# Attention norms over three engines, GpSimd's constants behind the norm, and a hint on the loop's back edge

## The reference

```python
def _layernorm(x, axis=-1, eps=1e-05):
    m = jnp.mean(x, axis=axis, keepdims=True)
    v = jnp.var(x, axis=axis, keepdims=True)
    return (x - m) / jnp.sqrt(v + eps)
...
    x = x + _L2_ffn_ref(_layernorm(x, axis=-1), L2_ffn_Wq, L2_ffn_bq, ...)
```

```python
        qkv = jnp.einsum('bsd,ed->bse', x, W_qkv)
        ...
        q = _rope(q, positions)
        k = _rope(k, positions)
        scores = jnp.einsum('bhqd,bhkd->bhqk', q, k) / jnp.sqrt(jnp.float32(dk))
        causal = jnp.tril(jnp.ones((S, S), dtype=bool))
        scores = jnp.where(causal[None, None, :, :], scores, -jnp.inf)
        attn = jax.nn.softmax(scores, axis=-1)
        out = jnp.einsum('bhqk,bhkd->bhqd', attn, v)
```

## Time and profile before

| | us |
|---|---|
| runs shown | 5552.94, 5564.20, 5540.51; median 5552.94 |
| profiled execution, its own time | 5545.3 |
| its span in the trace | 5543.6 |
| mean clock granted to TensorE | 0.921 of full speed |

### The profile page before, as it was taken

The page is one execution under the profiler, slowest core; times in us unless marked ns, Lnnn a source line. Parts: engine busy times, 40 slices in busy tenths (PEclk is TensorE's granted clock), DMA queues, the critical chain, the costliest instruction groups (busy, mean ns, idle before and its releaser), DMA issues. The chain is left out here.

```text
span 5543.6 us, 69676 instructions
## 1 busy us (share of the span) xinstructions
PE 4726.4 (85%) x22038; PEld 2207.0 (40%) x22038; DVE 3555.6 (64%) x8259; ACT 2738.1 (49%) x5070; POOL 1481.6 (27%) x1876
## 2 busy tenths in 40 slices
PE   4689887988879888898878988789887998989888
PEld 2134344443444324443244433444334543444344
DVE  5766856678556785667755587656865568456545
ACT  2255553555526554365542755435644455436453
POOL 2712620136101461105501064010730117200200
PEclk8889998999989999899989999999988999999789
DMA  3411310123101231012210132001320113101000
GB/s 130 146 35 60 115 62 1 47 67 107 53 3 54 73 110 35 3 54 92 91 34 4 53 113 84 20 23 45 119 74 13 35 50 118 67 2 54 1 27 6
DMA packets 150524, 315.98 MB, mean 57 GB/s; under 512 B 16208, under 2 KB 24912, under 8 KB 150112
## 3 DMA queue, kind: packets, MB, share of 16 engines
q1 hardware_dynamic: 150128, 311.17, 17.4%
HBM read 307.89 MB, written 3.21 MB: 56 GB/s over the span
## 5 line engine op out<-in xcount | busy, mean ns | idle before, releaser
L196 PE MATMUL BANKS<-WB 128*128 128x512 bf16 x1616 | 454.3, 433 | 194.1 <-DVE XN L440 56.5
L758 POOL TENSOR_TENSOR heads_work<-heads_work,heads_c_all 128x512 f32<-128x512 f32 x384 | 487.2, 1271 | 380.5 <-DVE heads_work L792 367.9
L1503 ACT ACTIVATE heads_prob<-BANKS 128x512 f32<-128x512 f32 (+3 forms) x768 | 377.3, 518 | 289.4 <-PE BANKS L1398 283.5
L212 POOL TENSOR_TENSOR rstd<-rstd,WF 128x4 f32<-128x4 f32 x24 | 24.2, 1007 | 1665.9 <-DVE rstd L230 1665.9
L725 PE MATMUL BANKS<-heads_work,WF 128*128 128x512 f32 x768 | 444.2, 664 | 0.4
L196 PEld LDWEIGHTS BANKS<-WB 128*128 128x128 bf16 x1616 | 166.7, 108 | 443.0 <-issue 216.7
L1398 PE MATMUL BANKS<-heads_parts_kT,heads_parts_qT 64*128 64x512 bf16 (+3 forms) x768 | 240.5, 363 | 69.3 <-DVE heads_nmax L1544 46.9
L405 POOL TENSOR_TENSOR rstd<-rstd,WF 128x4 f32<-128x4 f32 x48 | 48.5, 1010 | 936.7 <-DVE rstd L426 935.9
L2143 ACT COPY attn_probt<-BANKS 128x512 f32<-128x512 f32 x384 | 223.9, 583 | 126.1 <-PE BANKS L2069 123.7
L2164 DVE CUSTOM_DVE_ANT_0 attn_biased<-BANKS,attn_toep 128x512 f32<-128x512 f32 x384 | 263.1, 685 | 33.5 <-DMA attn_toep<-bias_line 20.4
L1541 DVE CUSTOM_DVE_ANT_0 BANKS<-BANKS,WF 128x384 f32<-128x384 f32 (+3 forms) x512 | 243.1, 503 | 64.0 <-PE BANKS L1398 60.9
(11 more groups left out here) (891 smaller groups left out, 10594.6 us busy)
## 6 DMA issues: line engine op xcount, KB each, us to landing
heads_c_all<-bc_rows SPq DMA_DIRECT2D x384, 256.0 KB, 3.2
heads_b_all<-bc_rows SPq DMA_DIRECT2D x192, 256.0 KB, 3.5
attn_toep<-bias_line SPq DMA_DIRECT2D x96, 448.0 KB, 4.3
last_x_w<-in_w SPq DMA_DIRECT2D x48, 512.0 KB, 3.6
s_c_all<-bc_rows SPq DMA_DIRECT2D x64, 256.0 KB, 3.3
yheads_c_all<-bc_rows SPq DMA_DIRECT2D x64, 256.0 KB, 3.2
s_b_all<-bc_rows SPq DMA_DIRECT2D x32, 256.0 KB, 3.6
yheads_b_all<-bc_rows SPq DMA_DIRECT2D x32, 256.0 KB, 3.5
```

What stands on the lines that cost most here:

```text
L196: nc.tensor.matmul(bank, ident_b, bc(ident_b[:, 0:1], [P, SEQ]), start=True, stop=True)
L758: nc.gpsimd.tensor_tensor(work[:, m % RW, :], work[:, m % RW, :], c_all[:, m % RC, :], ALU.mult).then_inc(rd, 1)
L1503: nc.scalar.activation(prob[:, i % PR, lo:hi], bank("T", i)[:, lo:hi], ACT.Exp).then_inc(exped, 1)
```

## The change

There are three parts. The two norms of the heads stage get `scaled_by_act=True`: VectorE only subtracts the mean, right behind the eps addition and with no wait for `rooted`, and sets a new semaphore `centred`; ScalarE waits for `centred` and `rooted` and multiplies the four tiles in place by `rstd`. The five memsets of the first attention get the due time of the projection, and wait for `ready`. And the loop is built with `hint_back_edge=True`.

```diff
@@ -392,11 +392,12 @@
             due[i] = next(streams[i], None)
 
     def norm_parts(st, tag, src, dst, small, at, dst_t=None, banks=None, rms=False, sq=None, gain_t=None, gain=None,
-                   shift=None, after=None, spare=None, idle=0, later=()):
+                   shift=None, after=None, spare=None, idle=0, later=(), scaled_by_act=False):
 
         s_stats, s_mv, s_rstd = small
         ch, normed, turned = st.sem(f"{tag}_chain"), st.sem(f"{tag}_normed"), st.sem(f"{tag}_turned")
         shifted, rooted, ready = st.sem(f"{tag}_shifted"), st.sem(f"{tag}_rooted"), st.sem(f"{tag}_ready")
+        centred = st.sem(f"{tag}_centred") if scaled_by_act else None
         HALF = SEQ // 2
 
         def gpsimd(pool):
@@ -424,9 +425,14 @@
                     last = V.bn_aggr(s_mv[:, j, :], s_stats[:, j, :])
                 link(last)
                 V.tensor_scalar(s_rstd[:, :], s_mv[:, :, 1], EPS, None, ALU.add).then_inc(shifted, 1)
-            yield at + 3.2
-            dve.wait_ge(rooted, 1)
-            for j in range(NJ):
+            if scaled_by_act:
+                for j in range(NJ):
+                    last = V.tensor_scalar(dst[:, j, :], src[:, j, :], s_mv[:, j, 0:1], None, ALU.subtract)
+                last.then_inc(centred, 1)
+            else:
+                yield at + 3.2
+                dve.wait_ge(rooted, 1)
+            for j in range(0 if scaled_by_act else NJ):
                 if rms:
                     ins = V.tensor_scalar(dst[:, j, :], src[:, j, :], s_rstd[:, j:j + 1], None, ALU.mult)
                 else:
@@ -464,6 +470,12 @@
         def scalar(act):
             if dst_t is None:
                 return
+            if scaled_by_act:
+                yield at + 3.2
+                act.wait_ge(centred, 1)
+                act.wait_ge(rooted, 1)
+                for j in range(NJ):
+                    nc.scalar.activation(dst[:, j, :], dst[:, j, :], ACT.Copy, scale=s_rstd[:, j:j + 1]).then_inc(normed, 1)
             yield at + 4.4
             act.wait_ge(turned, NJ // 2)
             if gain_t is not None:
@@ -1248,7 +1260,8 @@
                 pool.wait_ge(ready, 2)
                 nc.gpsimd.memset(parts[:, :, 0, :, SK:SM], 0.0).then_inc(blank, 1)
             else:
-                yield at - 5.0
+                yield at
+                pool.wait_ge(ready, 2)
                 nc.gpsimd.memset(vals[:, :, :, HD + 1:], 0.0)
                 nc.gpsimd.memset(vals[:, :, :, HD], 1.0)
                 nc.gpsimd.memset(parts[:, :, 0, :, SK:], 0.0)
@@ -1619,7 +1632,7 @@
                 ("a2", W("qkv2"), None, True, W("o2"), X, None),
                 ("a3", W("qkv3"), bqk_b, False, W("o3"), XN, W("bo3"))):
             ln = norm_parts(st, f"{tag}_ln", X, XN, SMALL, at, dst_t=XT, banks=(RING[1], RING[0]), after=before,
-                            spare=WEIGH, idle=10)
+                            spare=WEIGH, idle=10, scaled_by_act=True)
             rope = rope_parts(st, tag, ln.ready, w_qkv, bias, raw, RING, WEIGH, at + 6.0, bool(layers))
             head = head8_parts(st, tag, rope, heads, causal, O, RING, WEIGH, at + HEADS_AT, u)
             back = back_parts(st, f"{tag}_pb", head, O, ot[:, 0, :], w_o, add_to, RING, head.end + 0.5, bias=bias_o)
@@ -2243,7 +2256,7 @@
                 run(block, *streams)
 
     n = out.shape[0]
-    with nc.Fori(0, n - 2) as b:
+    with nc.Fori(0, n - 2, hint_back_edge=True) as b:
         layers(b, True, True)
     prefix[0] = "y"
     layers(n - 2, True, False)
```

## The result

| | kernel before | changed kernel |
|---|---|---|
| median of the first comparison, us | 5554.8 | 5481.6 |
| ratio, 95% interval | | 0.9867 (0.9840 to 0.9894) |
| median of a second comparison, us | 5540.7 | 5483.4 |
| ratio, 95% interval | | 0.9883 (0.9864 to 0.9902) |
| span of the profiled execution, us | 5543.6 | 5477.8 |

The account below looks back on a forecast made before the run. No engine is full, so hand-overs set the time. Hint 16.5, first norms 11.1, second norms 6.7 and clock 2 sum to 36.3 us, taking the median from 5552.9 to 5516 us, range 5502 to 5540.

Parts of the forecast that it names:

- The hint: Loop's five taken back edges: the branch hint saves 3.3 us at each, 16.5 us, bounds nothing to 17.5.
- First norms: Eight norms ahead of the first attention: projection 6.5 us after the statistics, gaining 11.1 us, bounds 5.6 to 24.
- the transposes start at about 4.9 ... whichever way the first step goes: First norm: TensorE's queue ends at 4.85 us, so pow and subtractions, side by side or in turn, leave projection at 6.5.
- Second norms: Eight norms ahead of the second attention: 7.7 us from seven, 1.0 lost in the last, sum 6.7, bounds 0.8 to 13.8.
- so I take 1.1: Second norm: pow and subtractions wait for each other, L1264 starts at 5.7 us, gain 1.1 us in each of seven.
- L1264 starts near 4.8: Second norm, case not taken: pow and subtractions run side by side, scaled tiles complete at 3.95 us, gain 2.0 us.
- I take +2: Clock term for the eight slow projections after a norm: a shorter TensorE stand gives back 2 us in all.
- bound of 13 for the clock: Upper bound of the clock term: up to 1.6 us per first norm, 13 us in all.
- the clock gives much more: Rival: slow projections go, 13 us in place of 2, some second norms side by side: 5503 us; chance 0.07.
- The late memset chain: Rival: moved memsets make mamba's L758 late, seven stages lose 3.7 us each: 5562, or 5579 without the hint; chance 0.05.
- The hint does nothing: Rival at the taken edges: the hint has no effect, 19.8 us are left, 5533 us; chance 0.16.
- the norms give nothing: Rival in the stages after norms: mamba waits or clock take back earlier projections, only the hint stays, 5536 us; chance 0.12.

Follow-up runs that it names:

- the scratch tiles: Kernel before with ScalarE scaling, memsets unmoved, no hint, plus four unread two-pointer VectorE tiles ahead of the subtractions; no total time given, tiles took 339 to 344 ns.
- the idle products: Kernel before with more than 10 idle products: 16 ahead of both norms, 5504.4 us, 0.9927; 22 in both, 0.9937; 22 in the second alone, 0.9942.
- their own kernels: Kernel before with the hint alone: 5524.9 us, 0.9984; changed kernel without the hint: 5485.6 us, 0.9914.

## Why the prediction missed

**The hint: right, with a remainder.** 14.9 us at the five taken edges against 16.5 forecast. The remainder behind it (about 5 us longer experts and bias attention) was not in the sum; the kernel as a whole gained 9 (0 to 18).

**First norms: the floor was read in one iteration and used for all.** The step that failed is "the transposes start at about 4.9 ... whichever way the first step goes". The 4.85 is the end of TensorE's queue in the first iteration, where the ten idle products ran at the low clock and took 4.42 us. Elsewhere in the kernel before three of the eight took 2.34, and after the change five of eight did. There the transposes follow ScalarE's tiles and the projection starts at 4.9, not 6.5: 5 × 1.65, with 2.3 us from the other three, is the 10.5 that were missing. The trace before holds the durations of all eight groups; the forecast rests on one.

**Second norms: the wrong one of two cases.** The step that failed is "so I take 1.1": L433 waits for whole GpSimd instructions beside it, and I put pow among these. The change and the scratch tiles show that pow on 128x4 holds nothing: 339 to 344 ns each beside it. The 3329 ns of the earlier trace rows stood beside five memsets in a row, none over 1.33 us; beside mamba's products L433 took up to 1431 ns. Neither says anything of pow. The other case of the same paragraph, "L1264 starts near 4.8", is what came, 4.83; counted to L1264, as the forecast did, the eight norms gave 13.3. The case that was taken also has a slip: 3.75 + 1.35 and the 0.85 that the first case puts behind its tiles are 5.95 and not 5.7, a gain of 0.85 and not of 1.1. The last sequence lost 0.2 us, the better end of 0.2 to 1.1. ScalarE's four tiles took 1.28 us, against 1.35.

**The clock: a term of 2 that was too small, and at the wrong place.** The step that failed is "I take +2", worked out for the products of the first norms alone. The four last rows of the table are −15.1 in one pair of executions and +4.1 in the other. So the size of the term is not known to better than that; on the medians 10 to 23 us are left beside edges and norms. The first attention can't carry it: in the sixteen profiled executions it lies between 834 and 862 us, and kernels with the old and with the new first norm overlap. What holds is the stretch behind the second norm, of which the forecast said nothing. It is 13.5 and 14.8 us shorter in the two executions; it took 2636 to 2656 us in the four kernels with the old norm and 4 or 10 products there, 2629 to 2638 in the five executions with the new one and 5 or 10, and 2601 to 2622 in the six with 16 or 22. The low-clock time in it fell from 498 to 464 us. From the first expert stage to the last store it fell from 772 to 687, and 43 of these 85 us lie in the norms and at the edges themselves. The sum's bound of 13 for the clock had the right size by luck, since it too was worked out for the first norms. That such a gain needs no earlier projection is shown by the idle products: they leave the second norm as long as it was, within 1.3 us in the sum of eight, and give 32 to 40 us. The rival of 0.07, "the clock gives much more", was nearest in kind and in size, and still 21 us short.

**The rivals.** The late memset chain fell with the memsets alone. "The hint does nothing" and "the norms give nothing" fell with their own kernels.

**What stays open.** The two edits and the idle products both shorten TensorE's stand in the second norm, and both remove its low-clock time. Between 4 and 10 products the stand shrinks by 1.30 us and next to nothing is gained, between 10 and 16 by 1.31 us, and 40 us are. Whether that step lies in the length of the stand or in the run of products ahead of it isn't shown: both change together, and no run takes them apart. Nor is it shown how low-clock stretches some 200 us behind the norm get shorter. In the kernel with the scratch tiles the second norms took 47.3 us, and the stretch behind them was still 2621.5, one execution.

## What to carry to other kernels

Where a wait of TensorE gets shorter, price what follows at the other level of the granted clock as well; here it was as large behind the second norm (13.5 us) as the gain in it (14.0). Take a second profiled execution before a stage's clock is priced: of one and the same kernel the first attention differed by 14 us. Read a queue's end at every repetition of the place, not at the first. And before a norm is rebuilt, try the number of idle products ahead of it: six more in one line gave the kernel before 40 us.

## What the runs showed of the hardware

A GpSimd pow on 128x4 took 1.01 us and did not hold VectorE's fp32 tensor_scalar from SBUF to SBUF, in either form; GpSimd memsets held both, up to 3329 ns for one of the two-pointer form and 1535 ns for one of the one-pointer form, where 0.34 and 0.28 us are the times beside pow. Two products of mamba (128x512) held the two-pointer form up to 1431 ns; no run has the other form beside them. ScalarE is held by neither: 0.38 to 0.40 us for a 128x128 tile scaled in place, four in 1.28 us. A taken back edge of this loop costs 6.1 to 7.1 us between the store and the next statistics without a hint, 3.7 to 3.9 with it (all sixteen traces), and 3.2 to 3.3 if it falls through; the hint itself takes 31 to 56 ns on each engine.
